# Attention stage: order of V's copy, x's halves and probability moves on VectorE and ScalarE

## What is computed

```python
q = layer_norm(query, ln1_g, ln1_b)
qh, kh, vh = (q @ wq + bq), (context @ wk + bk), (context @ wv + bv)    # 16 heads
scores = einsum("bqhd,bkhd->bhqk", qh, kh) / sqrt(32)
probs = softmax(where(allowed, scores, -inf))                           # allowed: key <= query
x = query + einsum("bhqk,bkhd->bqhd", probs, vh) @ wo + bo
out = x + gelu(layer_norm(x, ln2_g, ln2_b) @ w1 + b1) @ w2 + b2
```

## Time and profile before

| | |
|---|---|
| median of 3 runs | 2937.24 us (2937.08 to 2942.78) |
| profiled execution | 2934.94 us |
| its span, first to last instruction | 2933.2 us |
| TensorE busy | 2782.0 us, 95% |
| VectorE busy | 2030.9 us, 69% |
| ScalarE busy | 1657.2 us, 56% |
| GpSimd busy | 355.9 us, 12% |
| mean granted clock of TensorE | 0.985 |

### The profile page before, as it was taken

How to read it: one execution, slowest core, us unless ns; L and a number is a source line. 1 busy time by engine, 2 the same in 40 slices (tenths; PEclk the granted TensorE clock), 3 DMA queues, 4 the chain that set the end, 5 groups by cost and what they waited for, 6 DMA issues and landing times. The chain is left out here.

```text
span 2933.2 us, 65737 instructions
## 1 busy us (share of the span) xinstructions
PE 2782.0 (95%) x22056; PEld 2521.7 (86%) x22056; DVE 2030.9 (69%) x4884; ACT 1657.2 (56%) x4014; POOL 355.9 (12%) x364
## 2 busy tenths in 40 slices
PE   6999999999999999999984999999999999999999
PEld 4788777887778877788764999999999899999999
DVE  4777676766777667776657877787787766665566
ACT  3666666666666666566645456556555544444444
POOL 1211222112221122221210000000000000000000
PEclk9999999999999999999997999999999999999999
DMA  6667666676666666666634334434435344333342
GB/s 144 105 121 114 107 113 119 114 114 109 113 122 114 111 109 117 122 110 111 101 66 161 141 148 186 170 124 171 186 138 206 123 158 152 141 149 114 152 157 94
DMA packets 152506, 383.03 MB, mean 131 GB/s; under 512 B 12928, under 2 KB 17024, under 8 KB 144256
## 3 DMA queue, kind: packets, MB, share of 16 engines
q1 hardware_dynamic: 152448, 382.28, 53.6%
HBM read 172.51 MB, written 109.05 MB: 96 GB/s over the span
## 5 line engine op out<-in xcount | busy, mean ns | idle before, releaser
L726 ACT ACTIVATE sm<-sm,mins 128x128 f32<-128x128 f32 (+3 forms) x1024 | 571.6, 559 | 531.3 <-DVE mins L589 527.8
L589 DVE CUSTOM_DVE_ANT_0 sm<-bank_s,mask 128x128 f32<-128x128 f32 (+3 forms) x1024 | 479.5, 487 | 413.5 <-PE bank_s L441 404.4
L453 PE MATMUL bank_t<-ident,sm 128*128 128x128 f32 x2560 | 417.1, 277 | 47.0 <-DVE pT L536 32.9
L453 PEld LDWEIGHTS bank_t<-ident,sm 128*128 128x128 f32 x2560 | 303.1, 141 | 137.8 <-issue 45.6
L441 PE MATMUL bank_s<-stack 96*128 96x128 f32 (+3 forms) x1024 | 354.5, 387 | 7.0 <-DMA stack<-st_lo 7.0
L536 DVE COPY pT<-bank_t 128x384 f32<-128x384 f32 (+1 forms) x576 | 326.5, 567 | 0.5 <-PE bank_t L453 0.5
L1110 PE MATMUL bank_x<-b_hi,w_hi 128*128 128x256 f32 x1024 | 295.8, 289 | 23.6 <-DVE g L1311 9.6
L1110 PE MATMUL bank_x<-w_hi,a_hi 128*128 128x256 f32 x1024 | 291.7, 285 | 4.5 <-DVE a_lo L1230 4.5
L1112 PE MATMUL bank_x<-b_hi,w_lo 128*128 128x256 f32 x1024 | 291.6, 285 | 0.0
L1111 PE MATMUL bank_x<-b_lo,w_hi 128*128 128x256 f32 x1024 | 291.6, 285 | 0.0
L1111 PE MATMUL bank_x<-w_lo,a_hi 128*128 128x256 f32 x1024 | 291.3, 284 | 0.0
(11 more groups left out here) (178 smaller groups left out, 7411.7 us busy)
## 6 DMA issues: line engine op xcount, KB each, us to landing
stack<-st_hi SPq DMA_DIRECT2D x256, 256.0 KB, 6.1
stack<-st_lo SPq DMA_DIRECT2D x128, 256.0 KB, 7.4
xr<-x_scratch SPq DMA_DIRECT2D x32, 1024.0 KB, 6.0
b_scratch<-b_hi SPq DMA_DIRECT2D x16, 1792.0 KB, 9.9
b_scratch<-b_lo SPq DMA_DIRECT2D x16, 1792.0 KB, 13.9
b_hi<-b_scratch SPq DMA_DIRECT2D x16, 1792.0 KB, 7.4
b_lo<-b_scratch SPq DMA_DIRECT2D x16, 1792.0 KB, 11.2
xt<-in_x SPq DMA_DIRECT2D x64, 256.0 KB, 2.8
```

Of the source, the lines that this page charges most:

```text
L453: mm = pe.transpose(bank_t[n % 2][:, P * c:P * c + P], sm[:, n % SLOTS_S, P * c:P * c + P], ident[:])
L589: op = V.tensor_tensor_reduce(sm[:, n % SLOTS_S, off:off + w], bank_s[n % BANKS_S][:, off:off + w], mask[:, 512 - w:512], 1.0, 0.0, ALU.ad ...
L726: op = A.activation(row, row, ACT.Exp, bias=mins[:, g % 2, c:c + 1], scale=-1.0, accum_out=sums[:, g % 2, c:c + 1])
```

## The change

In the attention stage VectorE does a move ahead of a low half of x that is due at the same step. On ScalarE, where a V job and an x job end at the same step (V1b and X2 at step 9 of the third group), V's copy goes ahead of x's high half and the exponential. In the third group ScalarE also takes the moves of tiles 3 and 7. V1b's 24 products are spread 9, 9, 6 over steps 7 to 9 instead of 8, 8, 8. In the dense stage VectorE's add of C22 goes ahead of the normalisation of the next batch's last two tiles.

```diff
-ACT_MOVES = (5, 9, 11)
-
-
-def act_moves(k):
-
-    return k in ACT_MOVES
+ACT_MOVES = [(5, 9, 11), (5, 9, 11), (3, 5, 7, 9, 11), (5, 9, 11)]
+
+
+def act_moves(n):
+
+    g, k = divmod(n, 12)
+    return k in ACT_MOVES[g % 4]
...
-        [("Q3", {0: 6, 1: 6}), ("K3", {2: 6, 3: 6}), ("R", {4: 4}), ("V0b", {4: 8, 5: 8, 6: 8}), ("X0", {7: 4}), ("V1b", {7: 8, 8: 8, 9: 8}),
+        [("Q3", {0: 6, 1: 6}), ("K3", {2: 6, 3: 6}), ("R", {4: 4}), ("V0b", {4: 8, 5: 8, 6: 8}), ("X0", {7: 4}), ("V1b", {7: 9, 8: 9, 9: 6}),
...
+                    if (n > LAG and not it.tail or n <= LAG and not it.first) and not act_moves(n - LAG - 1):
+                        move_tile(dve, V.tensor_copy, it, n - LAG - 1)
                     for job, jg in it.ended(n):
                         if job[0] == "X":
                             x_low(it, job, jg, it.b + 1)
-                    if (n > LAG and not it.tail or n <= LAG and not it.first) and not act_moves((n - LAG - 1) % TG):
-                        move_tile(dve, V.tensor_copy, it, n - LAG - 1)
...
+                    x_ended = any(job[0] == "X" for job, _ in it.ended(n))
+                    for job, jg in it.ended(n):
+                        if job[0] == "V" and x_ended:
+                            v_copy(it, job, jg)
                     for job, jg in it.ended(n):
                         if job[0] == "X":
                             x_high(it, job, jg)
                     if not it.tail:
                         exponential(it, n)
-                    if (n > LAG and not it.tail or n <= LAG and not it.first) and act_moves((n - LAG - 1) % TG):
+                    if (n > LAG and not it.tail or n <= LAG and not it.first) and act_moves(n - LAG - 1):
                         move_tile(act, A.copy, it, n - LAG - 1)
...
-                        if job[0] == "V":
+                        if job[0] == "V" and not x_ended:
                             v_copy(it, job, jg)
...
                 a_low(c, 0, 0)
+                add(c, 0, "C22")
                 if norm:
                     normalise(c + 1, 2)
                     normalise(c + 1, 3)
-                add(c, 0, "C22")
```

## The result

The changed kernel takes **2893.7 us** (median, 2891.8 to 2898.4) against 2938.6 us of the kernel before in the same runs: ratio 0.9847, 95% interval 0.9830 to 0.9864. The profiled execution took 2891.79 us, 43.15 less than the one before.

The account below looks back on a forecast made before the run. TensorE's order of work sets the time, with stalls and clock falls. Gains 24.9 (batches) + 10.0 (clock) - 0.5 (last batch) + 8.3 (second stage) = 42.7 us off 2934.94 give 2892.2, plus 2.3 for the median: 2894.5 us, range 2885 to 2914.

Parts of the forecast that it names:

- V's copy: Third head group, ScalarE: with V's copy ahead, x's fourth transpose starts without a wait, 1.23 us earlier.
- T7: Transposes of tile 7's probabilities, third head group: held 0.4 us by ScalarE's move of tile 5.
- Move 6: VectorE's move of tile 6 ahead of x's low half, third group: tile 8's transposes come 2.2 us earlier.
- Move 7: Tile 7's move on ScalarE, third group: tile 9's transposes lose 0.55 us; left on VectorE, the sum is 8.3 us better.
- Move 3: Tile 3's move on ScalarE, third group: taken as 0.44 us long, not holding tile 5's transposes.
- The batches: Attention batches that prepare a next x: 1.66 us gained each, x 15 = 24.9 us; batch distance 89.8 us.
- The clock: Attention stage: TensorE's clock no longer falls after the third group's stalls, 10.0 us more; rival that it still falls, 0.20.
- The last batch: Attention batch without x: tile 7's move on ScalarE makes tile 9's transposes wait some 0.5 us longer, -0.5.
- The dense stage: Second stage: the add of C22 ahead of two normalisations saves 0.59 us in 14 iterations, 8.3 us; first iteration counted nothing.
- the wait only changes its name: Rival, third group: ScalarE's added moves hold tiles 7 and 9 as late as before; only 8.3 us left, 2929; chance 0.07.
- T9 doesn't wait: Rival, third group: tile 9's transposes aren't held, ScalarE's exponential and move being 0.5 us quicker; 2886; chance 0.09.

Follow-up runs that it names:

- e2: Kernel before with only V's copy put ahead of x's high half and the exponential on ScalarE: 2905.5 us, ratio 0.9896.
- e6: Changed kernel with V's copy alone put back behind the exponential and move on ScalarE: 2911.7 us, ratio 0.9914.
- e3: Kernel before with V's copy ahead on ScalarE and moves ahead of x's low halves on VectorE, nothing else: 2893.8 us, ratio 0.9854.
- e4: Changed kernel with the third group's move of tile 7 back on VectorE: 2884.6 us, ratio 0.9829.
- e8: Kernel of e4 with V1b's products spread 8, 8, 8 as before: 2889.3 us, ratio 0.9840.
- e1: Kernel before with the dense stage's edit alone, the add of C22 ahead of the normalisations: 2926.5 us, ratio 0.9964.
- e7: Kernel before with only the third group's moves of tiles 3 and 7 given to ScalarE: 2937.0 us, ratio 1.0002.
- e5: Kernel of e4 with the fourth group's move of tile 5 on VectorE instead of ScalarE: 2881.3 us, ratio 0.9814.

## Why the prediction was right

The forecast was 2894.5 us with a range of 2885 to 2914; measured 2893.7. By its own steps:

- **V's copy.** X3 was to come 0.26 us behind S10 and the copy to wait 0.1 us for V1b; measured 0.26 and 0.18. e2 and e6 show that the place of the copy alone makes and unmakes X3's wait (1.2 and 1.1 us per batch).
- **T7** was to be held 0.4 us by move 5. It stands 0.73 us behind X3, where the product behind X0 stands 0.35 behind it: 0.38.
- **Move 6.** T8 was to be 1.52 us behind X3; measured 1.48. From e2 to e3 the distance falls by 0.85 us: this is what the order on VectorE is worth once V's copy is ahead.
- **Move 7.** T9 was to be 4.09 us behind X3, 0.55 of it waiting; measured 4.10. e4 puts the price at 0.46 to 0.5 us per batch; with the last batch it is 9.9 us in the profiles and 9.1 between the medians, where the prediction said 8.3. This part of the change is a loss. Move 3 and the spread of V1b together are worth nothing: e3 without either has the distance of e4, and move 3 without the spread is a loss of 0.13 us (e8). Move 3 lasts 0.46 us, taken as 0.44.
- **The batches.** 14 distances were to fall from 91.5 or 92.9 to 89.8; they are 89.9, with one of 90.20, which is late by 0.27 at the first scores of a batch. Their 31.9 us are 14 x 1.6 = 22 from the waits (1.59 each, where the sum has 1.66) and about 10 from the clock, as in the sum.
- **The clock.** That it would stay up in the batches with an x held for all, and it was argued there from the fourth group only. What the runs add: with both waits it falls in part of the batches (the kernel before, e1, e7); with T8's and not X3's (0.88 us, e2) or X3's and not T8's (0.99, e6) it falls in none, and the distances don't alternate. I had weighed the idle time that is left; what the runs tell apart at this place is whether both waits, 2.5 us apart, are there, and one less is enough. The prediction has the clock low for some 2 us; the granted clock is 0.50 from 671.25 to 674.67, so for 3.4. Why only some of the batches are hit, 6 to 8 of 15, stays open. The single distances of 90.4 us in e5 and in e8 are no falls of the clock: there the first scores of a batch wait 1.40 and 0.57 us for a DMA.
- **The last batch was mis-sized.** Taken as a loss of 0.5 us; T9 waits 1.34 us there instead of 0.45, and the clock then falls to a mean of 0.73 from 1461 to 1480. The stretch from X3 of the fifteenth batch is 2.4 us longer where the sum has it about level; up to T4 of the last group the loss is 3.3 us (101.8 against 98.5, see e4). The step that failed is "there move 7 on ScalarE makes T9 wait some 0.5 us longer": the wait was 0.4 too low, and I had not asked whether the clock falls in a batch that has no X at all.
- **The dense stage.** 8.3 us forecast, 9.1 in the profile (14 x 0.65), 10.7 between the medians of e1, with 8.4 inside its interval. The first iteration gave nothing, as taken: its wait for the add fell from 2.98 to 2.08 us, but the wait for ScalarE's copy behind it rose from 0.59 to 3.00, while a further one of 1.60 went.
- **The start** is 3.4 us shorter already at X0 of the first batch (104.27 against 107.69), where the change hasn't begun; in the other profiles X0 stands at 105.6 to 110.4. That is the scatter of the start between executions. It covers the 2.4 us of the last batch, so that the total is closer than its terms, by luck.

Of the rivals, "the wait only changes its name" is true in part: half a microsecond per batch now stands at T9. "T9 doesn't wait" is what e4 gets by leaving move 7 where it was.

## What to carry to other kernels

Write the queues of the engines around a wait side by side and ask for each instruction in front of the late one whether anyone waits for it; here two swaps gave 1.2 and 0.85 us per batch without any work removed. Don't move work to the engine with the lower share because its share is lower: the two moves gained nothing alone, and the one that stood behind an exponential cost 0.5 us per batch and some 3 us in the last. And look at the batches that lack part of the pattern, the first and the last, by themselves.

## What the runs showed of the hardware

TensorE's granted clock fell to 0.50, its lower level, after two waits of 1.0 and 1.2 us that stand 2.5 us apart, in 6 to 8 of 15 batches (before, e1, e7), for 3.4 us and once for 6.8, at a cost of 1.4 and 2.9 us. It fell in no such batch where only one of the two was left (0.88 us in e2, 0.99 in e6). In the last batch equal waits, up to 1.59 us, left it up in e4 and were followed by a fall in e5: the waits alone don't decide it, and what else does, these runs don't show. The Trainium skill (TensorE: Matmul & The Clock Gate, HAM oscillation) describes such falls behind gaps in which TensorE waits for transfers; the trace agrees that idleness comes before each fall named here, in waits of 0.2 to 1.6 us for other engines.

A copy out of `bank_t` took ScalarE 0.46 us for 128x384 and 0.57 to 0.59 for 128x512, VectorE 0.55 and 0.69.
